# New positions for the chains' pieces in the order of every engine of a Mamba and attention kernel

## The reference

```python
# Mamba: x (time, 256) -> 512 channels, 16 states a channel
x_branch, z = split(x @ in_proj)
x_branch = silu(conv4(x_branch) + conv_b)
B_t, C_t, dt = split(x_branch @ x_proj); dt = softplus(dt * dt_proj + bias)
h = exp(dt * A) * h + dt * B_t * x_branch      # the scan over 1024 times
y = (sum_over_states(h * C_t) + D * x_branch) * silu(z)
out = y @ c_proj
# recurrent gate: over the four batch entries, one after another
f, i, c_new = sigmoid(...), sigmoid(...), tanh(...);  c = f * c + i * c_new
```

## Time and profile before

| what | value |
| --- | --- |
| median of 3 runs | 1269.98 us (1269.86 to 1270.35) |
| the profiled run's own time | 1271.65 us |
| its span, first to last instruction | 1270.1 us |
| mean granted TensorE clock | 0.984 |
| busy, share of the span | PE 90%, DVE 91%, POOL 77%, ACT 63% |
| HBM traffic | 301.73 MB read, 11.31 MB written |
| first scan to last scan | 99.9 to 1223.9 us |
| the eight slots | 143.0, 142.9, 142.8, 143.7, 142.8, 143.7, 140.8, 124.3 us |

### The profile page before, as it was taken

The page is one execution under the profiler, slowest core; times in us unless marked ns, Lnnn a source line. Parts: engine busy times, 40 slices in busy tenths (PEclk is TensorE's granted clock), DMA queues, the critical chain, the costliest instruction groups (busy, mean ns, idle before and its releaser), DMA issues.

```text
span 1270.1 us, 12563 instructions
## 1 busy us (share of the span) xinstructions
PE 1145.3 (90%) x3612; PEld 641.0 (50%) x3612; DVE 1159.2 (91%) x1136; ACT 794.3 (63%) x1443; POOL 980.9 (77%) x711
## 2 busy tenths in 40 slices
...
DMA packets 92308, 313.87 MB, mean 247 GB/s; under 512 B 10432, under 2 KB 15680, under 8 KB 91984
## 3 DMA queue, kind: packets, MB, share of 16 engines
...
HBM read 301.73 MB, written 11.31 MB: 246 GB/s over the span
## 4 chain that ended last, share of the span: by engine, by line
PE 46%; DVE 19%; POOL 16%; ACT 9%; issue 8%; DMA 2%; SPq 0%; DVEq 0%; POOLq 0%; ACTq 0%
PE ps L874 14%; DVE ps L1691 11%; POOL arena L1914 9%; PE ps L585 5%; PE ps L808 4%; PE ps L593 3%; PE ps L631 2%; DVE arena L1697 2%; PE ps L707 2%; PE ps L720 2%; PE ps L712 2%; PE ps L735 2%; ACT arena L898 2%; ACT ps L1254 2%; PE ps L728 1%
## 5 line engine op out<-in xcount | busy, mean ns | idle before, releaser
L1914 POOL TENSOR_TENSOR arena<-arena 128x1024 f32<-128x1024 f32 x255 | 600.7, 2364 | 139.9 <-PE ps L874 115.2
L1691 DVE TENSOR_TENSOR_SCAN ps<-ps,arena 128x1024 f32<-128x1024 f32 (+1 forms) x257 | 585.9, 2280 | 29.6 <-ACT ps L1254 16.7
L874 PE MATMUL ps<-arena,identF 128*128 128x512 f32 x1024 | 484.0, 604 | 46.7 <-DVE arena L1697 29.7
L1254 ACT ACTIVATE ps<-arena,negA 128x512 f32<-128x512 f32 x512 | 332.8, 684 | 89.6 <-DVE arena L1697 83.9
L874 PEld LDWEIGHTS ps<-arena,identF 128*128 128x128 f32 x1024 | 190.8, 193 | 266.6 <-issue 209.5
L1697 DVE TENSOR_TENSOR arena<-ps,arena 128x1024 f32<-128x1024 f32 x256 | 312.0, 1219 | 5.9
L889 ACT ACTIVATE arena<-arena,rnln 128x256 f32<-128x256 f32 x118 | 61.9, 590 | 42.5 <-POOL rnln L1724 25.7
L631 PE MATMUL ps<-arena,inw 128*128 128x512 f32 x128 | 60.0, 614 | 11.7 <-ACT arena L898 9.6
L712 PE MATMUL ps<-arena,inw 128*128 128x512 f32 x128 | 62.0, 608 | 3.3 <-DVE arena L1421 3.3
L1266 ACT ACTIVATE arena<-ps 128x2 f32<-128x2 f32 x128 | 22.1, 172 | 67.9 <-DVE arena L1697 67.4
L898 ACT ACTIVATE arena<-ps,modT 128x512 f32<-128x512 f32 x43 | 51.7, 1264 | 13.7 <-PE ps L458 11.6
...
## 6 DMA issues: line engine op xcount, KB each, us to landing
arena<-bc_scratch SPq DMA_DIRECT2D x511, 512.0 KB, 5.0
...
arena<-in_x SPq DMA_DIRECT2D x8, 512.0 KB, 8.9
xr_scratch<-arena SPq DMA_DIRECT2D x6, 512.0 KB, 6.7
px_scratch<-arena SPq DMA_DIRECT2D x6, 512.0 KB, 6.3
out_x<-arena SPq DMA_DIRECT2D x5, 512.0 KB, 2.6
...
woT<-in_woT SPq DMA_DIRECT2D x4, 512.0 KB, 9.4
```

The source lines that it names most:

```text
L874: x = pe.matmul(ps[:, Y, :], identF[:], inp[:, m % RING, q, :], start=False, stop=(i == BLOCK_STEPS - 1 and q == 1), skip_group_check=True)
L1254: x = act.activation(ps[:, 2 * (m % 2) + q, :], dt[:, kd, :], ACT.Exp, scale=negA[:, kd, 2 * i + q:2 * i + q + 1])
L1691: x = dve.tensor_tensor_scan(states, states, inp[:, m % RING, q, :].rearrange("p q t -> p (q t)"), 0.0, ALU.mult, ALU.add)
L1914: x = pool.tensor_tensor(inp[:, m % RING, :, :], u[:, kd:kd + 1, :].broadcast_to([P, 2, TH]), b_at[:, m % 3, :, :], ALU.mult)
```

## The change

Only the numbers in `TIMES` change. Every instruction stays, with its operands, its waits and its line; each engine has the same instructions in another order. The diff is nothing but rows of numbers; a few of them:

```diff
-    "sp_before": {"x_in": -7, "bc_out": 30.5, "dt_in": 30.5},
+    "sp_before": {"x_in": -8.5, "bc_out": 30.5, "dt_in": 30.5},
-    "sp_after": {"xr_out": 11.75, "px_out": 28.25},
+    "sp_after": {"xr_out": 18, "px_out": 26.25},
...
-    "pool_before": {"wo_gate": -5.75, "ffn_gate": -5.75, "ln1_rstd": -4.25, "ga_bias": 6.5, "op_add": (12, 12),
+    "pool_before": {"wo_gate": -7, "ffn_gate": -7, "ln1_rstd": -3.75, "ga_bias": 5.75, "op_add": (12, 12),
```

More of the change, by code:

```diff
@@ L44 @@
 TIMES = {
-    "sp_before": {"x_in": -7, "bc_out": 30.5, "dt_in": 30.5},
-    "sp_second": {"x_in": -21.5, "bc_out": 31.5, "dt_in": 31.5},
-    "sp_after": {"xr_out": 11.75, "px_out": 28.25},
[7 rows of a table removed]
[L55 to L72, removed]
@@ L73 @@
-    "dve_second": {"ln1_stats": -13.5, "ln1_moments": -11.25, "smax": (6.75, 9), "rsum": (9, 9.5),
[3 rows of a table removed]
-    "pool_before": {"wo_gate": -5.75, "ffn_gate": -5.75, "ln1_rstd": -4.25, "ga_bias": 6.5, "op_add": (12, 12),
[L78 to L82, removed]
@@ L83 @@
-    "pool_after": {"cp_gate": -7.25, "cp_add": (5, 5), "ln4_rstd": 6.75, "f_c": 21, "i_g": 25.5, "c_new": 25.5},
+    "sp_before": {"x_in": -8.5, "bc_out": 30.5, "dt_in": 30.5},
+    "sp_second": {"x_in": -23.5, "bc_out": 29.5, "dt_in": 29.5},
+    "sp_after": {"xr_out": 18, "px_out": 26.25},
[7 rows of a table added]
+        "gate_x": (12, 12.75, 17, 17.75, 21, 23.75), "gate_c": (12, 12.75, 17, 17.75, 21, 24.75), "px": (25.5, 26),
+        "om": 26},
+    "act_before": {"hn1": (-3.5, -3.5), "hB1": (-1.75, -1.75), "q0": -1.5, "k0": 1, "q1": 3.25, "exp0a": 3.75,
+        "exp0b": 3.75, "k1": 3.75, "v0": 7.25, "exp1a": 7.25, "exp1b": 7.25, "att0": 9.75, "v1": 9.75, "att1": 10.75,
+        "op_ev": (11.75, 12.75), "hn2": (14, 14), "q_scr": 17.75, "xdT": (20.25, 20.25), "ffn_ev": (21, 21),
+        "hn3": (23.5, 23.75), "hB3": (25, 25), "xc_init": (26, 26, 26.75, 26.75), "x_proj": 29,
+        "first_decay": (35, 38), "softplus": (34.25, 34.25), "dt_copy": 38, "xc_silu": 27.75},
@@ new lines @@
+    "act_second": {"hn1": (-10.25, -10.25), "hB1": (6, 6), "q0": 5.75, "k0": 5.75, "q1": 7.25, "exp0a": 7.25,
+        "exp0b": 7.25, "k1": 7.25, "v0": 9, "exp1a": 9.25, "exp1b": 9.25, "att0": 9.25, "v1": 10.25, "att1": 11.25,
+        "op_ev": (11.75, 12), "hn2": (14.25, 14.25), "q_scr": 18, "xdT": (20.25, 20.25), "ffn_ev": (20.5, 20.5),
+        "hn3": (24, 24), "hB3": (25.25, 25.25), "xc_init": (25.5, 25.5, 27.25, 27.25), "x_proj": 29.25,
+        "first_decay": (35.75, 39), "softplus": (31.5, 34.25), "dt_copy": 39, "xc_silu": 28},
```

13 lines of the change are left out of this document (added), and 20 rows, old and new, of the table TIMES.

## The result

The changed kernel is slower: median 1275.66 us (6 runs, 1274.75 to 1278.87) against 1269.92 us (6 runs) of the kernel before, a ratio of 1.0046 with a 95% interval of 1.0036 to 1.0056. That is 5.7 us more (5.8 by the ratio) where the text above forecast 1.2 us less; the time lies inside the range, near its upper end, and is what the second rival gives (1276). The profiled run took 1275.2 us with a span of 1273.8 us (before: 1271.65 and 1270.1).

The account below looks back on a forecast made before the run. A slot was taken as a loop of PE's and DVE's full stretches with hand-overs between. Gains of 9.0 us less 7.8 lost gave 1.2 us less than 1271.65: 1270.4, or 1268.8 as median; range 1259.0 to 1276.0.

Parts of the forecast that it names:

- the second rival: POOL's L1736, slots 0, 2, 4: woT lands at its old time in 2 and 4; stalls 15.1 us, total 1276; chance 0.20.
- What bounds the kernel: Each slot: DVE's and PE's full stretches and the hand-overs between them set its length; only pieces there are worth time.
- The loop: PE's full stretch, hand-over through POOL to DVE, DVE's full stretch, hand-over through POOL and ACT back to PE.
- The hand-over to PE: ACT's exponential table load leaves the layer norm's path to PE: 0.9 us gained in each of slots 1 to 5, 4.5 together.
- The quantization on POOL: Slots 2 and 4: bias pieces ahead of an inp fill POOL's 0.58 us wait for PE; 1.2 us gained together.
- Slot 6: Waits for the convolution's last tap (0.84 us) and a decay (0.68) go: 1.5 us gained, between 0 and 1.5.
- Slot 0: Earlier attention exponentials, a later reciprocal and a softplus cut in two shorten waits: 1.8 us gained.
- Slot 7: Order changes without moving a wait that could be found: 0.
- The stall: POOL's weight multiplications wait for woT ahead of inp(22), delaying DVE's scan: 7.8 us lost in slots 0, 2 and 4.
- The plain shift of the block: woT's landing moves exactly with the transfer block's earlier issue: scan late by 2.5, 3.4 and 4.6 us in slots 0, 2, 4.
- The row of C behind the block: The row for the product ahead of the stalled scan might come late; counted within the same stall, at no extra cost.

Follow-up runs that it names:

- e7: e4 with ln4's statistics (L1289) on DVE also put back behind scan 6; ratio 0.9957 to the kernel before.
- e6: e4 with POOL's forget-gate product (L1873) also put back ahead of the weight multiplications; ratio 0.9927 to the kernel before.
- e9: e8 with the first forget-gate piece on PE (L720, L728) also moved behind y(10); ratio 0.9931 to the kernel before.
- e8: The kernel before with only the moves of the hand-over to PE; ratio 0.9986 to the kernel before.
- e4: The changed kernel with POOL's weight multiplications (L1736), the transfer block and the residual store with its loads put back; ratio 0.9955 to the kernel before.
- e5: e4 with the store L405 also put back two steps; ratio 0.9949 to the kernel before.
- e10: e6 with the store L405 also put back; ratio 0.9932 to the kernel before.
- e2: The changed kernel with only the residual store and its loads (L396, L400, L401) put back six steps ahead; ratio 0.9994 to the kernel before.
- e3: The changed kernel with only the transfer block of halves 2 to 7 put back one step; ratio 1.0104 to the kernel before.

## Why the prediction was wrong

**What bounds the kernel** held. The loop passes a test that could have failed it: 6.5 us of DVE waits in PE's full stretch, taken away, changed nothing (e7), and 2.36 us of POOL at the hand-over of slots 2 and 4, taken away, gave 3.6 us in all (e6).

**The hand-over to PE** was forecast at 0.9 us a slot. The hand-over itself shrank by 1.8 to 2.0 us, more than the 1.28 of the table load that I took as its upper end. In slot 4 of the changed kernel, POOL's first piece (L1710) also starts 0.3 us sooner behind the aggregation (0.47 us against 0.78), and the copy of x_proj (L1095) no longer waits 0.17 us for PE. Of it, 1.3 to 1.6 us reach the slot where nothing interferes (e9). In the changed kernel slots 1, 3 and 5 gained 0.8, 2.0 and 1.4. The term's sign and mechanism were right, the size low. What I had not seen is that it needs the gate's move: without it (e8) all but slot 1 gave most or all of it back to the slower clock.

**The quantization on POOL**, 0.58 us in slots 2 and 4: it was not tried by itself, and no run here separates it.

**Slot 6** gained 0.8 of the 1.5 forecast. **Slot 0** was to gain 1.8 from its own tables. No run shows that gain: with the stall taken out it takes 143.3, 143.3, 142.4, 141.9 and 143.4 us in e4, e5, e6, e7 and e10, 142.9 in the mean; with the old tables it takes 143.0 before and 143.5 and 145.2 in e8 and e9. One order alone spreads over 1.4 us or more. **Slot 7**, set to zero, gained 2.3. The sum of the gains, forecast at 9.0, came out at 9.3 in e6 (0.9927). That it fits so well is luck in part: the hand-over, where nothing interferes, and slot 7 gave more than forecast, slot 6 less, and slot 0 is not known.

**The stall** is the step that failed, and it is a term that was mis-sized, not a mechanism that was missed. The prediction named the place, the wait and the three slots. It took 7.8 us (3.1, 3.1 and 1.6). In the trace the scan and the product ahead of it waited 2.73, 4.82 and 6.76 us in slots 0, 2 and 4, 14.3 together. Putting the three moves back gave 11.5 us, and with L1873, whose cost the stall had covered, 15.1. Against gains of 9.3 that is the 5.8 us of the result. The number came from a choice: a row lands 5.0 us after its issue in the median, and the block drains at 320 GB/s. In slot 4 the B row went out at 756.77, and by this rule woT had to land at 756.8 + 5.0 + 6.5 = 768.3; it landed at 772.85, 4.5 us later. The rate was right on average, 318 GB/s from the block's issue on. The bytes were not: up to 768.3 the rule has 3.6 MB move at its rate, and 5.0 MB moved until woT landed. The store and the loads of the same change, 1.18 MB, stood ahead of it, and e2 prices them at 4.0 us in slot 4 and at about 1 in slot 2. I had written them down at 3.7 us each and used them for the upper bound alone. The rule could have been tried on the kernel before, which has no store there: it gives 758.2 + 11.5 = 769.7 in slot 4 and 185.0 + 11.5 = 196.5 in slot 0, and woT landed at 771.2 and 199.6. It was 1.5 and 3.1 us short already. The plain shift of the block gave 10.5 us, nearer to the truth than the value I took below it. The second rival, by which the earlier issue gives nothing in slots 2 and 4, gave 15.1 us, at a chance of 0.20. Slot 4 went by it to 0.2 us.

**The row of C behind the block** was counted as covered by the same stall. e3 bears this out: with that row in time the scan still waits 9.15 us.

**L1873**, one step later on POOL, got no price at all. I had looked at it as a piece that makes room for the inp; it left a wait in which it was free and went where POOL is full, for 3.6 us once the stall is gone (e6 against e4).

The Trainium skill's fit of 2.0 us plus the bytes at 436 GB/s (DMA: Bandwidth & Descriptors, Anatomy of one DMA, for the other kind of issue) gives an estimate of 3.2 us for woT; the trace now has 12.1, further from it than the 9.8 of before. The fit is for one transfer, and the measurement decides here.
